# Single precision attention scores, merged second-layer weights and a new step order in a two-layer transformer kernel

## The reference

```python
# layer 0
xn = layernorm(x)
Q, K, V = heads of xn @ Wq.T, xn @ Wk.T, xn @ Wv.T      # 16 heads of 8; Q and K divided by their norms
c = clip(Q @ K.T, -0.999, 0.999)
W = (1 - arccos(c) / pi) ** 16;  W = W / (sum(W) + 1e-6)
a1 = (W @ V) @ Wo.T + bo
q, k, v = heads of xn @ W_qkv + b_qkv
a2 = softmax(q @ k.T / sqrt(8)) @ v
gate = softmax(xn @ W_gate + b_gate), the two largest kept   # 8 experts
a3 = sum over experts of gate_e * (xn @ W_e + b_e)
x = x + a1 + a2 + a3
# layer 1
xn = layernorm(x)
q, k, v = xn @ w_qkv.T                                    # one head of 128, causal
x2 = x + (softmax(q @ k.T / sqrt(128), causal) @ v) @ w_out.T
h = silu(fp4(xn) @ fp4(w_gate).T) * (fp4(xn) @ fp4(w_up).T)   # 352 columns, blocks of 16
x = x2 + fp4(h) @ fp4(w_down).T
```

## Time and profile before

| | |
|---|---|
| median of 3 runs | 2048.47 us (2047.59 to 2049.12) |
| the profiled execution | 2050.03 us, span 2048.2 us |
| TensorE matmuls busy | 1625.1 us, 79% |
| VectorE busy | 1790.3 us, 87% |
| ScalarE busy | 1875.9 us, 92% |
| GpSimd busy | 1062.5 us, 52% |
| mean granted TensorE clock | 0.92 |
| transfers | 5 GB/s over the span |

### The profile page before, as it was taken

One profiled execution on the slowest core, in us unless ns is written; L12 is line 12 of the kernel. 1 busy time (PEld: TensorE's weight loads), 2 busy tenths in 40 slices (PEclk: granted clock), 3 DMA queues, 4 the chain that ended last, 5 costly groups with the idle time before them and its releaser, 6 DMA issues.

```text
span 2048.2 us, 39684 instructions
## 1 busy us (share of the span) xinstructions
PE 1625.1 (79%) x12405; PEld 796.0 (39%) x12405; DVE 1790.3 (87%) x4071; ACT 1875.9 (92%) x2144; POOL 1062.5 (52%) x448
## 2 busy tenths in 40 slices
PE   2678788888888888888888888888888888887865
PEld 1233444433444443344444334444433444443433
DVE  5778989999998999999899999989999998998844
ACT  2399999999999999999999999999999999999991
POOL 1455555456555545655554565555456555545520
PEclk9979999999999999999999999999999999999875
DMA  1000000000000000000000000000000000000000
GB/s 41 4 4 1 6 6 0 5 6 5 6 5 6 0 5 6 5 6 5 6 0 5 6 5 6 5 6 0 5 6 5 6 5 6 0 5 7 4 4 6
DMA packets 21059, 11.21 MB, mean 5 GB/s; under 512 B 1431, under 2 KB 20953, under 8 KB 20956
## 3 DMA queue, kind: packets, MB, share of 16 engines
q1 hardware_dynamic: 20956, 10.20, 1.7%
HBM read 6.00 MB, written 4.19 MB: 5 GB/s over the span
## 4 chain that ended last, share of the span: by engine, by line
ACT 40%; DVE 23%; issue 22%; PE 13%; POOL 1%; DVEq 1%; ACTq 1%; SPq 0%; DMA 0%; POOLq 0%
ACT curve L532 21%; ACT root L532 7%; ACT prob L532 3%; PE psM L1167 3%; DVE nmax L858 3%; DVE curve L848 3%; PE psM L1004 2%; ACT L563 2%; ACT L636 1%; PE psV L1199 1%; DVE h L421 1%; ACT hqT L532 1%; POOL qk L514 1%; PE psM L1151 1%; DVE hqT L417 1%
## 5 line engine op out<-in xcount | busy, mean ns | idle before, releaser
L532 ACT ACTIVATE curve<-curve 128x2048 f32<-128x2048 f32 x384 | 717.7, 1902 | 4.8 <-POOL curve L503 3.4
L500 POOL TENSOR_TENSOR root<-curve 128x2048 f32<-128x2048 f32 x128 | 460.1, 3600 | 426.1 <-DVE curve L852 425.9
L532 ACT ACTIVATE root<-root 128x2048 f32<-128x2048 f32 x256 | 484.4, 1905 | 8.1 <-POOL root L500 7.8
L503 POOL TENSOR_TENSOR curve<-curve,root 128x2048 f32<-128x2048 f32 x64 | 348.8, 5452 | 93.3 <-ACT root L532 93.3
L852 DVE TENSOR_SCALAR curve<-psS 128x1024 f32<-128x1024 f32 x256 | 306.0, 1216 | 25.3 <-PE psS L1035 19.1
L858 DVE TENSOR_REDUCE nmax<-psS 128x4 f32<-128x1024 f32 x256 | 308.8, 1214 | 7.2 <-PE psS L1044 6.9
L1199 PE MATMUL psV<-prob,vf 128*32 128x256 f32 x2048 | 270.8, 425 | 3.9 <-ACT prob L532 0.6
L532 ACT ACTIVATE prob<-psS 128x1024 f32<-128x1024 f32 x256 | 261.3, 1021 | 11.8 <-PE psS L1065 11.0
L1199 PE MATMUL psV<-curve,vc 128*32 128x256 f32 x2048 | 225.4, 408 | 40.0 <-ACT curve L532 36.3
L520 POOL TENSOR_TENSOR stk<-qk,stk 128x512 f16<-128x512 f32 x128 | 168.4, 1325 | 155.3 <-ACT stk L532 155.3
L848 DVE TENSOR_TENSOR curve<-curve,root 128x2048 f32<-128x2048 f32 x64 | 177.7, 2777 | 5.6 <-ACT root L532 5.6
(11 more groups left out here) (190 smaller groups left out, 2856.9 us busy)
## 6 DMA issues: line engine op xcount, KB each, us to landing
xt<-in_L_attn_x SPq DMA_DIRECT2D x32, 128.0 KB, 2.2
out<-yo SPq DMA_DIRECT2D x32, 128.0 KB, 1.8
we<-in_L_ffn_W_experts SPq DMA_DIRECT2D x1, 512.0 KB
curve<-in_L_attn_w_qkv SPq DMA_DIRECT2D x1, 192.0 KB
curve<-in_L_ffn_w_down SPq DMA_DIRECT2D x1, 176.0 KB
curve<-in_L_ffn_w_gate SPq DMA_DIRECT2D x2, 64.0 KB
curve<-in_L_ffn_w_up SPq DMA_DIRECT2D x2, 64.0 KB
curve<-in_L_ffn_W_qkv SPq DMA_DIRECT2D x1, 128.0 KB
```

The source lines that it names most:

```text
L500: nc.gpsimd.tensor_tensor(root[:, two], curve[:, p, two], curve[:, p, two], ALU.mult).then_inc(s_sq, 1)
L503: nc.gpsimd.tensor_tensor(curve[:, p, two], curve[:, p, two], root[:, two], ALU.mult).then_inc(s_half[0], 1)
L532: return nc.scalar.activation(out, in_, func, **kw)
```

## The change

- The scores are computed in single precision. The split into high and low parts (stages high, stack) and the tensors `stk`, `stkT`, `mstk` go. The queries stand as they are, four heads in 32 rows; the keys are written into `kpad`, which holds zeros in the rows of the other three heads (`own_rows`). Stages qT and kT transpose them (2 and 8 transposes for each of the two kinds, 20 in all) and VectorE copies them out of six banks. The maxima stay in single precision: two transposes, and the second product of e picks the head's row (`pick`).
- In setup w_q and w_k of layer 1 are multiplied with each other, and w_v with w_out. p1 has one product where it had two, stage w1 goes, and o1 adds straight to x1. The row sum of the softmax comes from a column of ones in `v1`, and the accumulator reads and stage rs1 go.
- The half-angle products of pairs 0, 2 and 3 are on GpSimd, only pair 1 is on VectorE. The squares for the norms go from ScalarE to GpSimd (qsq), and unit is two operations.
- hT transposes all of `h` (padded with zeros to 384 columns), and ScalarE copies once where it copied twice.
- `SCHEDULE` is in a new order, with other lags for some stages.

```diff
-HALF_ON_DVE = (1, 3)
+HALF_ON_DVE = (1,)
 SCHEDULE = [
...
+    ("table", 0, -1), ("wln", 0, -1), ("s1e", 0, -2), ("quanth", 1, -2), ("m", 7, 0), ("quanth", 2, -2),
+    ("choose", 5, 0), ("wln", 1, -1), ("wln", 2, -1), ("experts", 0, 0), ("quanth", 3, -2), ("c", 5, 0),
+    ("quanth", 4, -2), ("wexp", 0, -1), ("residual", 0, 0), ("c", 6, 0), ("pvw", 0, -1), ("wexp", 1, -1),
+    ("wln", 3, -1), ("maxT", 0, 0), ("wexp", 2, -1), ("pvw", 1, -1), ("finf", 0, -1), ("ln0", 0, 1), ("pvw", 2, -1),
+    ("quanth", 5, -2), ("experts", 1, 0), ("pvw", 3, -1), ("rstd0", 0, 1), ("wexp", 3, -1), ("e", 0, 0), ("sq", 0, 0),
+    ("p1T", 0, -2), ("pvw", 4, -1), ("pvw", 5, -1), ("ln", 0, 0), ("xnT", 0, 1), ("c", 7, 0), ("sq", 1, 0),
+    ("pvw", 6, -1), ("quanth", 6, -2), ("oC", 0, -1), ("pvw", 7, -1), ("ln", 1, 0), ("e", 1, 0), ("o1", 0, -2),
+    ("finc", 0, -1), ("e", 2, 0), ("pvf", 0, 0), ("proj", 0, 1), ("e", 3, 0), ("pvf", 1, 0), ("ocT", 0, -1),
+    ("quanth", 7, -2), ("quanth", 8, -2), ("proj", 1, 1), ("gmax", 0, 1), ("ln", 2, 0), ("gexp", 0, 1), ("pvf", 2, 0),
+    ("wo", 0, -1), ("e", 4, 0), ("sq", 2, 0), ("ln1", 0, -1), ("norm", 0, 1), ("rstd1", 0, -1), ("choose", 0, 1),
+    ("e", 5, 0), ("pvf", 3, 0), ("guess", 0, 1), ("ln", 3, 0), ("xn1T", 0, -1), ("pvf", 4, 0), ("quantx", 0, -1),
+    ("sq", 3, 0), ("choose", 1, 1), ("fadd", 0, -1), ("newton", 0, 1), ("quantx", 1, -1), ("quantx", 2, -1),
+    ("e", 6, 0), ("quantx", 3, -1), ("e", 7, 0), ("choose", 2, 1), ("table", 1, 0), ("quantx", 4, -1), ("sigm", 0, 0),
+    ("qsq", 0, 1), ("choose", 3, 1), ("quantx", 5, -1), ("kT", 0, 1), ("qT", 0, 1), ("choose", 4, 1), ("unit", 0, 1),
+    ("quantx", 6, -1), ("qT", 1, 1), ("quantx", 7, -1), ("sigm", 1, 0), ("sigm", 2, 0), ("quantx", 8, -1),
+    ("kT", 1, 1), ("m", 0, 1), ("pvf", 5, 0), ("mul", 0, 0), ("c", 0, 1), ("hT", 0, -2), ("load", 0, 1), ("c", 1, 1),
+    ("hT", 1, -2), ("mul", 1, 0), ("mul", 2, 0), ("p1", 0, -1), ("m", 1, 1), ("arctan", 0, 0), ("pvf", 6, 0),
+    ("xqT", 0, -1), ("gu", 0, -1), ("hmul", 0, -1), ("pvf", 7, 0), ("sigm", 3, 0), ("m", 2, 1), ("m", 3, 1),
+    ("s1", 0, -1), ("oF", 0, 0), ("m", 4, 1), ("arctan", 1, 0), ("c", 2, 1), ("arctan", 2, 0), ("gu", 1, -1),
+    ("c", 3, 1), ("m", 5, 1), ("hmul", 1, -1), ("c", 4, 1), ("quanth", 0, -1), ("arctan", 3, 0), ("down", 0, -2),
+    ("m", 6, 1), ("mul", 3, 0),
 ]
...
-        stk = sb("stk", [P, 4, NT * HEADS, SLOTS, HD], F16)
-        stkT = sb("stkT", [P, 4, 4, T], F16)
+        qT = sb("qT", [P, 2, T])
+        kT = sb("kT", [P, 2, 4, T])
...
+                if stage == "qsq":
+                    pool.wait_ge(s_nsum, due(s_nsum, b - 1))
+                    pool.wait_ge(s_qkc, due(s_qkc, b))
+                    cos = qk[:, :, :, :, :].rearrange("p k j h d -> p (k j h) d")
+                    nc.gpsimd.tensor_tensor(qsq[:, :, :], cos, cos, ALU.mult).then_inc(s_qsq, 1)
...
-                            ins = mm(psS[:, slot, a, kt, :], stkT[rows(hh), 1, g, kt * P:(kt + 1) * P], stkT[rows(hh), 0, g, :],
+                            ins = mm(psS[:, slot, a, kt, :], kT[rows(hh), COS, g, kt * P:(kt + 1) * P], qT[rows(hh), COS, :],
                                      start=True, stop=True)
...
-                            mm(psS[:, slot, a, kt, :], stkT[rows(hh), 3, g, kt * P:(kt + 1) * P], stkT[rows(hh), 2, g, :],
+                            mm(psS[:, slot, a, kt, :], kT[rows(hh), SOFT, g, kt * P:(kt + 1) * P], qT[rows(hh), SOFT, :],
                                start=True, stop=False)
-                            ins = mm(psS[:, slot, a, kt, :], onesb[rows(hh), :], mT[rows(hh), g, :], start=False, stop=True)
+                            ins = mm(psS[:, slot, a, kt, :], pick[rows(hh), g, :], mT[rows(hh), :], start=False, stop=True)
...
-                    for m in range(2):
-                        ins = mm(bank[:, m * T:(m + 1) * T], w1T[:, m, :], xn1T[:, :], start=True, stop=True)
-                    ins.then_inc(s_p1p, 1)
+                    mm(bank[:, 0:T], wqk1[:, :], xn1T[:, :], start=True, stop=True).then_inc(s_p1p, 1)
```

More of the change, by code:

```diff
@@ L41 @@
 UNITS, UC = 8, 1024
-SLOTS = 4
-HALF_ON_DVE = (1, 3)
+HALF_ON_DVE = (1,)
 FULL_GROUP = 32
-KINDS = (2, 3, 0, 1)
+SOFT, COS = 0, 1
 SCHEDULE = [
[L54 to L75, removed]
@@ L80 @@
 USES = {"xnT": 1, "proj": 2, "maxT": 1, "finc": 1, "ocT": 1, "wo": 1, "xn1T": 1, "p1": 2, "s1": 1, "p1T": 1, "o1": 1,
-        "w1": 1, "xqT": 1, "gu": 2, "finf": 1, "stackT": 1, "experts": 2, "hT": 1, "down": 1}
+        "xqT": 1, "gu": 2, "finf": 1, "qT": 1, "kT": 2, "experts": 2, "hT": 1, "down": 1}
 MISC = [(s, a, use) for s, a, lag in SCHEDULE for use in range(USES.get(s, 0))]
@@ L342, in build @@
         for j in range(NT):
-            READ[("proj", j, 0)], READ[("proj", j, 1)] = (s_qkc, 2 * j + 2), (s_qkf, 3 * j + 3)
+            READ[("proj", j, 0)], READ[("proj", j, 1)] = (s_qkc, 2 * j + 2), (s_qkf, 4 * j + 4)
             READ[("gu", j, 0)], READ[("gu", j, 1)] = (s_hg, j + 1), (s_h, j + 1)
             READ[("experts", j, 0)], READ[("experts", j, 1)] = (s_moe, 8 * j + 7), (s_moe, 8 * j + 8)
-            READ[("hT", j, 0)] = (s_hT, 2 * j + 2)
-        for kind in range(4):
-            READ[("stackT", kind, 0)] = (s_stkT, kind + 1)
+            READ[("hT", j, 0)] = (s_hT, j + 1)
+        for kind in range(2):
+            READ[("qT", kind, 0)] = (s_qT, kind + 1)
+            READ[("kT", kind, 0)], READ[("kT", kind, 1)] = (s_kT, 2 * kind + 1), (s_kT, 2 * kind + 2)
         def bank_read(stage, arg, use, t, uses=MISC):
@@ L374, in build @@
         TRANSPOSES += [(wload[:, 3, :], woT[:, :])]
-        TRANSPOSES += [(wload[:, 4 + k, :], w1T[:, k, :]) for k in range(3)]
         TRANSPOSES += [(wload[:, 7, :], wout1T[:, :])]
@@ L399, in fp4 @@
         def fp4(eng, src, dst, scratch, s_steps, b, step):
[L401 to L403 removed]
             a, r, e = scratch
[L405 to L406 removed]
+            if len(src.shape) == 2:
+                rows, nb = src.shape[0], src.shape[1] // BLOCK
+                z = src.rearrange("p (n k) -> p n k", k=BLOCK)
+                o = dst.rearrange("p (n k) -> p n k", k=BLOCK)
+                a, r, e = a[0:rows, 0:nb], r[0:rows, 0:nb], e[0:rows, 0:nb, :]
+            else:
+                z = src.rearrange("p j (n k) -> p j n k", k=BLOCK)
+                o = dst.rearrange("p j (n k) -> p j n k", k=BLOCK)
+            n, last = o, len(z.shape) - 1
             eng.wait_ge(s_steps, due(s_steps, b, step))
@@ L843, in run @@
                         dve.wait_ge(s_e, due(s_e, b - 1))
-                    nc.vector.tensor_copy(stkT[:, kind, :, :], bank16[k]).then_inc(s_stkT, 1)
+                if stage == "qT":
+                    bank, k = misc_bank(stage, arg, 0)
+                    dve.wait_ge(s_qTp, due(s_qTp, b, arg + 1))
+                    nc.vector.tensor_copy(qT[:, arg, :], bank[:, 0:T]).then_inc(s_qT, 1)
+                if stage == "kT":
+                    for use in range(2):
+                        bank, k = misc_bank(stage, arg, use)
+                        dve.wait_ge(s_kTp, due(s_kTp, b, 2 * arg + use + 1))
+                        nc.vector.tensor_copy(kT[:, arg, 2 * use:2 * use + 2, :],
+                                              bank[:, :].rearrange("p (i t) -> p i t", i=2)).then_inc(s_kT, 1)
                 if stage == "mul" and arg in HALF_ON_DVE:
```

276 lines of the change are left out of this document (126 added, 150 removed).

## The result

| | before | after |
|---|---|---|
| median | 2048.11 us | 2574.57 us |
| ratio | | 1.258, interval 1.255 to 1.261 |
| span of the profiled execution | 2048.2 us | 2572.5 us |
| one step of the loop | 59.7 us | 76.6 us |

The forecast was 2298 us, with a range of 2080 to 2460. The direction was right, the bound too; the size was not, and the range missed. Where the executions of one kernel differ by more than 1.5%, its ratio to before is taken from the faster ones. The page of the changed kernel: busy time, the granted clock, and the costliest groups that matter (line, operation, count, busy us, mean ns, then idle time before and its releaser).

A forecast was written before the change was run, and what follows sets the result against it. TensorE was taken to become the bound: 49.4 us a step plus the changes gave 64.1, with 3.4 of gaps 67.5, +7.8 over 59.7; 32 batches add 250, forecast 2298 us, range 2080 to 2460.

The forecast's parts named there:

- The bound: TensorE, at 64.1 us of work a step, replaces ScalarE as the largest; ScalarE falls to 53.3 busy.
- The price of single precision: Score products on TensorE: +10.1 us a step for c and m, +10.5 for e, before neighbours' overlap.
- A score unit: On TensorE, a c or m unit goes from 0.36 to 0.99 us, an e unit from 0.54 to 1.85.
- the forecast's other terms: TensorE outside the scores, per step: clock -2.9, transposes +0.5, row maxima -0.3, p1 -0.5, w1 -0.6.
- Neighbours: Neighbouring score units on different TensorE strips overlap, returning 3 x 0.8 and 2 x 1.7 = 5.8 us; half counted, 2.9.
- The rule on weight loads: TensorE loads take columns over 1.2 ns; one at a time, neighbours gain nothing and the sum is 67, not 64.
- The clock: TensorE, busier, runs at 2.4 GHz throughout: -2.9 us a step, bounds 0 and -2.9.
- Gaps: TensorE's idle time per step: a third of today's 10.3 us, 3.4, above all at kT and qT.
- Rival 3: VectorE waits at the norms for GpSimd's squares; 5 us of gap a step gives 2458 us; chance 0.08 above 2450.
- The sum: TensorE's 64.1 us of work plus 3.4 of gaps make a step of 67.5, +7.8, over 32 batches +250.
- What ScalarE loses: Copies, squares and accumulator reads leave ScalarE: 5.0 us a step, to 53.3 busy.
- Rival 1: ScalarE stays the bound: scores under 18 us a step on TensorE, step 54.7, time 1888 us; chance 0.14.

The follow-up runs named there:

- e11: The changed kernel's arithmetic in the order of the kernel before, half-angle products of pairs 1 and 3 on VectorE: 2426.55 us, executions scattering from 2378 to 2476.
- e13: e11 with c, m and e in half precision, low parts left out: 2001.12 us, ratio to before 0.977.
- e1: The changed kernel with p1 moved ahead of the half-angle products of pairs 1 and 2: 2438.97 us, ratio to before 1.191.
- e7: The kernel before with only the second-layer merge, column of ones, one hT copy and squares on GpSimd: 2088.92 us, ratio 1.022.
- e3: The changed kernel, its order kept, with c, m and e in half precision, low parts left out: 2166.93 us, ratio to before 1.059.
- e5: The changed kernel with both half precision c, m and e and p1 moved as in e1: 2191.06 us, ratio to before 1.070.

## Why the prediction was wrong

- *The bound.* Right. TensorE became the bound, ScalarE's and VectorE's waits for the scores are where they were forecast. The price of single precision was nearly right as work: +17.7 forecast for the scores (20.6 less half the neighbours' overlap), +18.7 measured in one order (e11 against e13).
- *A score unit.* Taken from the column strips of pv at 0.99 and, for e, at 1.85; measured 1.06 and 2.03. Times 16 and 8 that is 2.6 us a step. Without the clock's share the changed kernel needs 66.9 (e1), against 64.1. Of the 2.8 between them the neighbours take 1.2 off again (next point), and 1.3 stands outside the scores: with half precision scores TensorE has 46.9 a step (e13), where the forecast's other terms give 49.4 - 2.9 + 0.5 - 0.3 - 0.5 - 0.6 = 45.6.
- *Neighbours.* A pair of e units is 3.01 instead of 4.06, so strips do overlap, but the saving is 1.05 and not 1.7. A pair of c or m units that finds both buffers free takes 1.0 to 1.2 (in e1, x16 at 1091.68 in 1.16), a saving of about 1.0 and not 0.8; in e1 m 2 and 3 do not overlap (1075.39 to 1077.58). Together that is some 4.1 us a step in e1, where half of 5.8 was counted. The rule on weight loads of the Trainium skill ("TensorE: Matmul & The Clock Gate", "LDWEIGHTS (loading the stationary operand)"), read as loads one at a time, would need 32 x 0.107 = 3.4 us for the pair of e units, an estimate by its figure. The trace has 3.01, so the loads do not run one at a time here; the last section has their row.
- *The clock.* The term -2.9 for a TensorE at 2.4 GHz throughout was wrong in the changed kernel (0.93) and right once the one long wait was gone (1.00 in e1's stretch). It was taken at its favourable bound, and it hung on the next term: 3.1 us.
- *Gaps.* This is the step that failed most: "I take a third, 3.4". It was 6.5, and with the clock the one wait at gu makes 5.2 us (4.2 over the whole run) of the 9.1 that a step was short. The forecast followed GpSimd's product into ScalarE's chain only; it did not ask what two engines do that multiply side by side, nor what stands behind VectorE's product on VectorE: a copy that frees a PSUM bank, for which TensorE waits. Rival 3 asked the right kind of question at another place, the norms, where VectorE does not wait for GpSimd in the changed kernel. The row that shows this in advance is the second product of GpSimd in the trace of before, 6.37 us where the first takes 4.53; only its mean, 5449 ns, had been read the earlier trace rows.
- *The sum.* 67.5 + 2.8 work + 3.1 clock + 3.1 gaps = 76.5; 16.9 us more than before, times 32 is 541, measured on the span 524. The runs lead from one kernel to the other like this: 2048 before; 2001 with the other edits and half precision scores in the old order (e13); 2427 with single precision (e11); 2575 with the new order and pair 3's product on GpSimd, of which the copy ahead of one product returns 136 (e1).
- *What ScalarE loses.* 5.0 forecast, 3.5 measured (58.3 to 54.8 a step), as in e7: the durations of short queued instructions overcount.
- *Rival 1.* Its point of decision was roughly right as a sum, but its end was not. "Under 18 ScalarE sets the step again" at 54.7: with half precision the step is 64.7 in the new order and 58.0 in the old one. The order and the place of pair 3's product carry 5 to 7 us a step between them, and the forecast gave them nothing. It is not the wait at gu, which comes to 5.9 us in e3; what it is stays open.

## What to carry to other kernels

Where an order is laid for one engine as the bound, ask for each long instruction what is queued behind it on its engine and which bank or buffer that frees; a copy moved ahead of one product gave 5% here. A saving on the engine that is full is not a gain until the next one's total has been added up, and a single precision product cost TensorE four half precision ones of the same columns (0.43 against 0.11 us for 256). Here several engines were within 10% of the step, and the sum of none of them gave the time: taking work off ScalarE made the kernel slower in e7, and the move that gave 5% with single precision scores gave nothing with half precision in e5. Before a move is carried over, look whether the wait that it removes is there.
